# Loads, turned weights and row scales of the first layer in one block, and both square roots taken early

## The chip, the cores and the metric

The kernel runs on one core of a Trainium2 chip, as one launch. The metric is the device time of a run in microseconds (us). Five engines work side by side, each through its own list of instructions, and wait for each other through semaphores: PE (TensorE, matrix products and transposes), DVE (VectorE), ACT (ScalarE), POOL (GpSimd) and SP (SyncE, which only starts DMA transfers here). ACT starts transfers too.

## What is computed

The reference is a stack of eight layers on x of 16 sequences of 256 tokens with 128 features. Every layer begins with some normalisation of each token's row. The change lies in the beginning of the first layer, a selective state-space layer, and in the row scales that six of the layers compute. Cut to that:

```
# first layer (L0_attn_a): applied to x after a plain normalisation
mu  = mean(x, -1); var = var(x, -1)
xn  = (x - mu) * rsqrt(var + 1e-5) * norm_g + norm_b
xz  = xn @ in_w.T                       # 512 columns: x_, z
u   = silu(conv_b + causal_conv(x_, conv_w))          # 4 taps
dbc = u @ xproj_w.T                     # 64 + 16 + 16 columns
delta = softplus(dbc[:, :64] @ dt_w.T + dt_b)
A   = -exp(A_log)
h_t = exp(delta_t*A)*h_(t-1) + delta_t*B_t*u_t;  y_t = h_t . C_t
out = ((y + u*D) * silu(z)) @ out_w.T + residual
# a mixture layer later on (L0_ffn): 8 experts, chosen by feats @ centroids.T
```

A layer of this stack sees the row already normalised once (scale 1/sqrt(var+eps)) and normalises it again, so a row has two scales: `rstd`, and `rnorm`, the product of both. The second one needs the variance of the row once normalised, var/(var+1e-5), and its own root.

## The kernel before, in words

The 4096 tokens lie in 32 tiles of 128 rows (`env.X`, 128 partitions x 32 x 128). Work is written in blocks: in a block each engine has its own list, and at the block's end all engines meet in a barrier before the next block begins.

The program begins with five blocks. `launch` (L312 to L343): SP starts the eight transfers of X, four tiles each, ACT starts eight transfers of constant tables (`ident`, `identb`, `causal`, `causalT`, `ranks`, `steps`, `firsts`, `sel`; `sel` has 768 KB) and waits for them, and DVE takes each tile's statistics with bn_stats as its part lands. `row_scales` (L178 to L209, called at L471): SP starts fifteen transfers of the first layer's weights and vectors and waits for all; DVE works out the scales (`scale_rows`, L135), ACT takes the two square roots (`root_rows`, L166). A block of its own (L487 to L500): ACT forms A = -exp(A_log), DVE takes the mean off the centroids. `turn_weights` (L101 to L131): PE turns twelve pieces of the weights through `ident` into PSUM, DVE and ACT copy them out in turn. Then the first block of real work, `ma`: DVE normalises tiles into `ma_rows` (L364), PE turns them (L580) and multiplies (L588, L596, L604, L612), DVE convolves (L553, L558), ACT applies the nonlinearities.

`scale_rows` has ten steps, or seventeen with a second scale. The order before: four groups up to var+1e-5 (L139 to L146), wait for root 1, `rstd` (L148), `keep`, `shift`, then three steps that multiply the variance twice by `rstd` (L154 to L156), wait for root 2, a maximum with `floor` (L158), reciprocal (L159), `root` (L160), `rnorm` (L161). It is used in the beginning of the program, in `experts` (twice, names e_), in `begin` for `attention` (b2f) and `product_keys` (k5f and k7f), and with one scale only for rotary (r4sc) and state space (s6f). In `experts` ACT takes the roots between the copies of a loop that scores the tokens (L1278 to L1284). In `begin`, ACT takes both roots and then copies weights out of PSUM (L291).

## Time and profile before

| | us |
|---|---|
| median of 3 runs | 2678.5 (2677.33 to 2682.02) |
| profiled execution, its own time | 2683.2 |
| its span | 2681.5 |
| first tile written by `ma` begins | 30.33 |
| second expert layer begins | 1081.9 |

The profiled execution is 4.7 us above the median and 1.7 us of its time lie outside the span. Times in the rows below are from the beginning of the span. A row of the timeline is: start, time until the end of the last instruction in it, engine, line, operation, output<-inputs, how many, and in brackets how long the engine stood idle before and what ended that. SPq and ACTq are the times in which the engine's queue issued transfers.

### The profile page before, as it was taken

To read this page: it belongs to the slowest core of one execution; us is meant where nothing else is said; L and a number is where in the kernel's file an instruction comes from. 1 tells how busy PE (TensorE), PEld (TensorE's weight loads), DVE (VectorE), ACT (ScalarE), POOL (GpSimd) and SP (SyncE) were. 2 spreads that over 40 slices of the span, in tenths; PEclk is the share of its full clock that TensorE was granted. 3 is DMA by queue.
4 is the path that set the end of the run, shared out by engine and by line. 5 is a ranking of instruction groups with operands and counts; after the bars stand their busy time and mean duration, and the time that the engine had idled before them with its cause. 6 is when DMAs were issued, how large, how long until landed. Compare 5 with 4: busy or idle time off the path is not lost. (4 is left out here: it accounts for less than half of the span.)

```text
span 2681.5 us, 59371 instructions
## 1 busy us (share of the span) xinstructions
PE 2094.4 (78%) x17450; PEld 1739.1 (65%) x17451; DVE 2254.2 (84%) x5549; ACT 1864.0 (70%) x4275; POOL 1617.8 (60%) x1472
## 2 busy tenths in 40 slices
PE   4748888879599999693488877888888447888888
PEld 2336666658488888573466656777777326777777
DVE  6489999875588888656888857999999788999998
ACT  3579999756555555463255547999999349999997
POOL 0069999717300000274555547999999209999997
PEclk9869999989899999796799998999999769999999
DMA  2013333241200000111100000000000000000000
GB/s 60 3 48 97 97 96 97 72 143 52 64 1 0 0 0 1 48 52 42 41 2 0 0 1 1 0 0 0 0 0 0 1 0 1 4 8 4 4 4 8
DMA packets 67879, 70.65 MB, mean 26 GB/s; under 512 B 10408, under 2 KB 46464, under 8 KB 67648
## 3 DMA queue, kind: packets, MB, share of 16 engines
q1 hardware_dynamic: 61632, 57.56, 7.5%
q0 software_dynamic: 4992, 10.23, 1.4%
q10 hardware_dynamic: 1120, 1.22, 0.2%
q8 instruction: 65, 1.06, 0.2%
q14 instruction: 70, 0.57, 0.1%
HBM read 57.32 MB, written 11.67 MB: 26 GB/s over the span
## 5 line engine op out<-in xcount | busy, mean ns | idle before, releaser
L1899 POOL TENSOR_TENSOR k5a_psums<-k5a_sims 128x1024 f32<-128x1024 f32 x224 | 421.7, 1914 | 16.2 <-DVE k5a_w L2107 12.0
L1899 POOL TENSOR_TENSOR k7a_psums<-k7a_sims 128x1024 f32<-128x1024 f32 x224 | 421.7, 1915 | 12.9 <-DVE k7a_w L2107 8.7
L994 POOL TENSOR_TENSOR mc_hc<-mc_h,mc_cs 128x512 f32<-128x512 f32 x256 | 328.0, 1297 | 32.7 <-DVE mc_h L961 17.3
L1964 PE MATMUL k5a_pw<-g_ident,k5a_w 128*128 128x128 f32 x2048 | 265.6, 277 | 70.4 <-DVE k5a_hid L2115 45.9
L1964 PE MATMUL k7a_pw<-g_ident,k7a_w 128*128 128x128 f32 x2048 | 262.0, 276 | 70.1 <-DVE k7a_hid L2115 45.9
L1964 PEld LDWEIGHTS k5a_pw<-g_ident,k5a_w 128*128 128x128 f32 x2048 | 226.8, 141 | 113.7 <-DVE k5a_w L2107 52.7
L961 DVE TENSOR_TENSOR_SCAN mc_h<-mc_dA,mc_inj 128x512 f32<-128x512 f32 x256 | 298.5, 1200 | 2.3 <-PE mc_inj L850 1.8
L1964 PEld LDWEIGHTS k7a_pw<-g_ident,k7a_w 128*128 128x128 f32 x2048 | 227.3, 141 | 109.4 <-issue 63.8
L2107 DVE SCALAR_TENSOR_TENSOR k7a_w<-k7a_psums,k7a_best,k7a_lift 128x1024 f32<-128x1024 f32 x224 | 279.5, 1272 | 0.5 <-ACT k7a_lift L2035 0.3
L2107 DVE SCALAR_TENSOR_TENSOR k5a_w<-k5a_psums,k5a_best,k5a_lift 128x1024 f32<-128x1024 f32 x224 | 279.1, 1270 | 0.5 <-ACT k5a_lift L2035 0.3
L2035 ACT ACTIVATE k7a_lift<-k7a_psums 128x1024 f32<-128x1024 f32 x224 | 229.2, 1023 | 37.5 <-DVE k7a_w L2107 33.2
L2035 ACT ACTIVATE k5a_lift<-k5a_psums 128x1024 f32<-128x1024 f32 x224 | 228.4, 1020 | 33.3 <-DVE k5a_w L2107 28.9
L1341 POOL MEMSET e_keep<- 128x256 f32 x2 | 0.6, 312 | 407.6 <-POOLq L35 407.6
L850 PE MATMUL mc_inj<-g_ident,mc_bdu 128*128 128x128 f32 x1024 | 167.9, 287 | 58.0 <-DVE mc_h L961 53.9
L906 ACT ACTIVATE mc_bdu<-mc_duT,m_BT 128x256 f32<-128x256 f32 x384 | 178.5, 497 | 16.4 <-PE mc_inj L850 13.9
L2491 ACT ACTIVATE r4a_pr<-r4a_pst 128x384 f32<-128x384 f32 x256 | 111.6, 488 | 111.0 <-PE r4a_pst L2647 109.8
L850 PEld LDWEIGHTS mc_inj<-g_ident,mc_bdu 128*128 128x128 f32 x1024 | 109.9, 142 | 112.0 <-DVE mc_h L961 108.9
L914 ACT ACTIVATE mc_dA<-m_delta,m_A 128x510 f32<-128x510 f32 x256 | 181.2, 708 | 0.4 <-DVE mc_h L961 0.3
L2557 POOL TENSOR_SCALAR_AFFINE_SELECT r4a_pr<-r4a_pr 128x256 f32<-128x256 f32 x256 | 101.0, 412 | 110.5 <-ACT r4a_pr L2491 110.5
L1719 ACT ACTIVATE b2a_pr<-b2a_psc,b2a_nm 128x128 f32<-128x128 f32 x128 | 47.3, 369 | 158.0 <-DVE b2a_nm L1767 135.1
L857 PE MATMUL mc_yT<-g_ident,mc_hc 128*128 128x128 f32 x1024 | 153.6, 273 | 1.3 <-POOL mc_hc L994 1.1
L2764 DVE TENSOR_REDUCE r4a_nm<-r4a_work 128x2 f32<-128x512 f32 (+1 forms) x192 | 121.8, 682 | 14.0 <-PE r4a_work L2618 13.0
(515 smaller groups left out, 5869.9 us busy)
## 6 DMA issues: line engine op xcount, KB each, us to landing
mc_cs<-c_rows SPq DMA_DIRECT2D x128, 256.0 KB, 3.1
e_w<-in_L_ffn_W_dram SPq DMA_DIRECT2D x16, 256.0 KB, 5.3
token_rows<-e_zn SPq DMA_DIRECT2D x16, 256.0 KB, 3.6
e_zn<-token_out SPq DMA_DIRECT2D x16, 256.0 KB, 5.1
g_X<-in_L_attn_a_x_dram SPq DMA_DIRECT2D x8, 256.0 KB, 5.7
out_dram<-g_X SPq DMA_DIRECT2D x7, 256.0 KB, 2.3
e_zs<-token_rows,e_token POOLq DMA_INDIRECT x78, 2.6
token_out<-e_ys,e_token POOLq DMA_INDIRECT x78, 2.3
```

The costliest lines, as they stand in the source:

```text
L850: ins = nc.tensor.transpose(inj[:, q % RI, k * P:(k + 1) * P], bdu[:, S % 2, k, h * P:(h + 1) * P], env.ident[:, :])
L857: ins = nc.tensor.matmul(yT[:, n % 2, h, k * P:(k + 1) * P], rows[:, k * P:(k + 1) * P], env.ident[:, :], start=(first and k == 0), stop=( ...
L906: ins = nc.scalar.mul(bdu[:, S % 2, k, :], duT[:, n % 2, k, :], BT[:, n * TPC + k, st:st + 1])
L914: nc.scalar.activation(dA[:, q % RA, :, 1:SEQ], d[:, :, 1:SEQ], ACT.Exp, scale=A[:, h, st:st + 1]).then_inc(decay, 1)
L961: nc.vector.tensor_tensor_scan(h_[:, q % RB, :], dA[:, q % RA, :, :].rearrange("p s t -> p (s t)"), inj[:, q % RI, :], 0.0, ALU.mult, ALU. ...
L994: nc.gpsimd.tensor_tensor(hc[:, q % RH, :], h_[:, q % RB, :], cs[:, S % RC, :], ALU.mult).then_inc(outs, 1)
L1899: nc.gpsimd.tensor_tensor(psums[:, h - 1, :, :], rows_of(p, h), s2, ALU.add).then_inc(pooled, 1)
L1964: ins = nc.tensor.matmul(pw[:, j, :], w[:, h % WR, j * P:(j + 1) * P], env.ident[:, :], start=(h == 0 and j % 4 == 0), stop=(h == HD - 1 a ...
L2035: nc.scalar.activation(lift[:, h % LR, :], sums_of(h), ACT.Relu).then_inc(lifted, 1)
L2107: nc.vector.scalar_tensor_tensor(w[:, h % WR, :], sums_of(h), best[:, p, h, 7:8], lift[:, h % LR, :], ALU.is_ge, ALU.mult).then_inc(weighe ...
L2491: nc.scalar.activation(pr[:, h, :, :].rearrange("p b c -> p (b c)"), pst[:, h % 2, 0:3 * P], ACT.Exp).then_inc(expd, 1)
L2764: nc.vector.tensor_reduce(dst, src, AX, ALU.max, negate=True).then_inc(maxed, 1)
```

## The change

The five beginning blocks up to `ma` become one, `opening`. In it SP starts four parts of X, then A_log, the centroids with their two companions, dt_w, the six small vectors, then the five tables that are left; ACT starts `ident`, the other four parts of X, then in_w, xproj_w, out_w and b1. Each kind of load has its own semaphore, and each user waits for its own. `sel`, `causalT` and `root`, which nothing reads, are gone. The block waits for the weights and the small vectors; the tables are waited for at the end of `ma`. The mean of the centroids moves from DVE (a reduction and two steps) to POOL (nine steps that halve the row). PE's transposes are grouped: six places in PSUM, each copied out by ACT alone. A is formed by ACT ahead of the roots.

In `scale_rows` the variance of the normalised row is worked out as var * 1/(var+1e-5), which needs no root; these three steps stand ahead of the first wait for ACT. The maximum is left out where `floor` is zero (all but attention), `root` is left out. The steps are 15, or 16 in attention.

```diff
@@ -144,35 +144,46 @@
     link(nc.vector.scalar_tensor_tensor(t3, t1, 0.25, t1, ALU.mult, ALU.mult))
     link(nc.vector.scalar_tensor_tensor(t0, t2, 1.0 / P, t3, ALU.mult, ALU.add))
     link(nc.vector.tensor_scalar(t1, t0, 1e-5, None, ALU.add))
+    assert link.n == VARIANCE
+    if second:
+        k, eps, floor, gain = second
+        link(nc.vector.reciprocal(t3, t1))
+        link(nc.vector.tensor_tensor(t4, t0, t3, ALU.mult))
+        link(nc.vector.tensor_scalar(t0, t4, float(k), float(eps), ALU.mult, ALU.add))
+        assert link.n == SQUARES
     dve.wait_ge(rooted, 1)
     link(nc.vector.reciprocal(env.rstd[:, :], t2))
     link.inc(nc.vector.tensor_scalar(env.keep[:, :], env.rstd[:, :], 1.0, None, ALU.add))
-    link(nc.vector.scalar_tensor_tensor(env.shift[:, :], env.mean[:, :], -1.0, env.rstd[:, :],
-                                        ALU.mult, ALU.mult))
+    link.inc(nc.vector.scalar_tensor_tensor(env.shift[:, :], env.mean[:, :], -1.0, env.rstd[:, :],
+                                            ALU.mult, ALU.mult))
     if second:
-        k, eps, floor, gain = second
-        link(nc.vector.tensor_tensor(t1, t0, env.rstd[:, :], ALU.mult))
-        link(nc.vector.tensor_tensor(t3, t1, env.rstd[:, :], ALU.mult))
-        link(nc.vector.tensor_scalar(t1, t3, float(k), float(eps), ALU.mult, ALU.add))
         dve.wait_ge(rooted, 2)
-        link(nc.vector.tensor_scalar(t4, t2, float(floor), None, ALU.max))
+        if floor:
+            link(nc.vector.tensor_scalar(t4, t4, float(floor), None, ALU.max))
         link(nc.vector.reciprocal(t3, t4))
-        link.inc(nc.vector.tensor_scalar(env.root[:, :], t4, 1.0 / gain, None, ALU.mult))
-        link(nc.vector.scalar_tensor_tensor(env.rnorm[:, :], t3, float(gain), env.rstd[:, :],
-                                            ALU.mult, ALU.mult))
-    assert link.n == (17 if second else 10)
+        link.inc(nc.vector.scalar_tensor_tensor(env.rnorm[:, :], t3, float(gain), env.rstd[:, :],
+                                                ALU.mult, ALU.mult))
+    assert link.n == scale_steps(second)
+
+
+VARIANCE, SQUARES = 7, 10
...
+def scale_steps(second):
+
+    if second is None:
+        return VARIANCE + 3
+    return SQUARES + (6 if second[2] else 5)
 
 
 def root_rows(nc, act, vec, rooted, tmp, second):
 
-    t1, t2 = tmp[:, 1, :], tmp[:, 2, :]
-
-    act.wait_ge(vec, 7)
-    nc.scalar.activation(t2, t1, ACT.Sqrt).then_inc(rooted, 1)
+    act.wait_ge(vec, VARIANCE)
+    nc.scalar.activation(tmp[:, 2, :], tmp[:, 1, :], ACT.Sqrt).then_inc(rooted, 1)
     if second:
 
-        act.wait_ge(vec, 13)
-        nc.scalar.activation(t2, t1, ACT.Sqrt).then_inc(rooted, 1)
+        act.wait_ge(vec, SQUARES)
+        nc.scalar.activation(tmp[:, 4, :], tmp[:, 0, :], ACT.Sqrt).then_inc(rooted, 1)
...
+def opening(nc, env, x_dram, ident, first, rest, negated, centring, turns, tables):
...
+        def bring(eng, q):
+            eng.dma_start(env.X[:, q * G:(q + 1) * G, :], rows[:, q * G:(q + 1) * G, :]).then_inc(x_in[q], 16)
+
+        def fetch(eng, j):
+            for dst, src in first[j]:
+                eng.dma_start(dst, src, allow_slow_non_contiguous=True).then_inc(fetched[j], 16)
+
         @block.sync
         def _(sp):
-            for q in range(PARTS):
-                sp.dma_start(env.X[:, q * G:(q + 1) * G, :], rows[:, q * G:(q + 1) * G, :]).then_inc(loaded[q], 16)
+            for q in range(0, PARTS, 2):
+                bring(sp, q)
+            for j in range(1, len(first), 2):
+                fetch(sp, j)
+            for dst, src in rest:
+                sp.dma_start(dst, src, allow_slow_non_contiguous=True).then_inc(small_in, 16)
+            for dst, src in tables[1]:
+                sp.dma_start(dst, src).then_inc(tables[0], 16)
+            sp.wait_ge(small_in, 16 * len(rest))
+
+        @block.tensor
+        def _(pe):
+            pe.wait_ge(ident_in, 16)
+            for j, (ready, pieces, places) in enumerate(turns):
+                if ready is None:
+                    pe.wait_ge(centred, CENTRED)
+                    pe.wait_ge(fetched[3], 16 * len(first[3]))
+                else:
+                    pe.wait_ge(fetched[ready], 16 * len(first[ready]))
+                for src, c0 in pieces:
+                    p, f = src.shape[0], src.shape[1]
+                    ins = nc.tensor.transpose(turned[0:f, j, c0:c0 + p], src, env.ident[0:p, 0:p])
+                ins.then_inc(placed, 1)
 
...
+            act.dma_start(*ident).then_inc(ident_in, 16)
+            for q in range(1, PARTS, 2):
+                bring(act, q)
+            for j in range(0, len(first), 2):
+                fetch(act, j)
+
+            def evacuate(j):
+                act.wait_ge(placed, j + 1)
+                for dst, c0 in turns[j][2]:
+                    f, n = dst.shape[0], dst.shape[1]
+                    ins = nc.scalar.copy(dst, turned[0:f, j, c0:c0 + n])
+                ins.then_inc(evacuated, 1)
+
+            at, A = negated
+            act.wait_ge(fetched[at], 16 * len(first[at]))
+            nc.scalar.activation(A, A, ACT.Exp).then_inc(raised, 1)
+            act.wait_ge(raised, 1)
+            nc.scalar.mul(A, A, -1.0).then_inc(raised, 1)
+            act.wait_ge(vec, VARIANCE)
+            nc.scalar.activation(tmp[:, 2, :], tmp[:, 1, :], ACT.Sqrt).then_inc(rooted, 1)
+            evacuate(0)
+            act.wait_ge(vec, SQUARES)
+            nc.scalar.activation(tmp[:, 4, :], tmp[:, 0, :], ACT.Sqrt).then_inc(rooted, 1)
+            for j in range(1, len(turns)):
+                evacuate(j)
+            act.wait_ge(evacuated, len(turns))
+
+        @block.gpsimd
+        def _(pool):
+            at, cent = centring
+            link = Link(pool, centred)
+            pool.wait_ge(fetched[at], 16 * len(first[at]))
+            n = P // 2
+            link(nc.gpsimd.tensor_tensor(csum[0:E, 0:n], cent[:, 0:n], cent[:, n:2 * n], ALU.add))
+            while n > 1:
+                n //= 2
+                link(nc.gpsimd.tensor_tensor(csum[0:E, 0:n], csum[0:E, 0:n], csum[0:E, n:2 * n], ALU.add))
+            link(nc.gpsimd.tensor_scalar(csum[0:E, 0:1], csum[0:E, 0:1], 1.0 / P, None, ALU.mult))
+            link(nc.gpsimd.tensor_scalar(cent, cent, csum[0:E, 0:1], None, ALU.subtract))
+            assert link.n == CENTRED
...
         @block.vector
         def _(dve):
             for q in range(PARTS):
 
-                dve.wait_ge(loaded[q], 16)
+                dve.wait_ge(x_in[q], 16)
                 for i in range(q * G, (q + 1) * G):
                     nc.vector.bn_stats(env.stats[:, i, :], env.X[:, i, :]).then_inc(done, 1)
             dve.wait_ge(done, NT)
+            link = Link(dve, vec)
+            scale_rows(nc, env, dve, link, rooted, tmp, second)
+            link.wait()
...
+            first = [
+                [(in_w[:, :, :], a["in_w"].rearrange("(j p) c -> p j c", p=P))],
+                [(A[:, :, :], a["A_log"].rearrange("(h p) s -> p h s", p=P))],
+                [(xp[:, :], a["xproj_w"])],
+                [(rows3[0:E, :], ffn["centroids"]), (rows3[E:2 * E, :], ffn["gamma"]), (rows3[2 * E:3 * E, :], ffn["beta"])],
+                [(ow[:, :], a["out_w"])],
+                [(dtw[:, :, :], a["dt_w"].rearrange("(h p) r -> p h r", p=P))],
+                [(rows1[:, :], ffn["b1"].rearrange("e (j p) -> (e j) p", p=P))]]
...
+            turns = [
+                (0, [(in_w[:, j, :], j * P) for j in range(4)], [(wx[:, :], 0), (wz[:, :], DI)]),
+                (2, [(xp[:, h * P:(h + 1) * P], h * 96) for h in range(H)], [(xprojT[:, :, :].rearrange("p h r -> p (h r)"), 0)]),
+                (5, [(dtw[:, h, :], h * P) for h in range(H)], [(dtT[:, :], 0)]),
+                (4, [(ow[:, h * P:(h + 1) * P], h * P) for h in range(H)], [(outT[:, :, :].rearrange("p h c -> p (h c)"), 0)]),
+                (6, [(rows1[:, :], 0)], [(env.b1[:, :, :].rearrange("p e j -> p (e j)"), 0)]),
+                (None, [(rows3[:, :], 0)], [(env.byexpert[:, :, :].rearrange("p a e -> p (a e)"), 0)])]
+            opening(nc, env, a["x"], ident, first, rest, (1, A[:, :, :]), (3, rows3[0:E, :]), turns, (tabled, tables))
...
@@ -1280,8 +1354,8 @@
                     lower(n - 1)
                 if n < 2:
 
-                    act.wait_ge(scaled, (7, 13)[n])
-                    nc.scalar.activation(tmp[:, 2, :], tmp[:, 1, :], ACT.Sqrt).then_inc(rooted, 1)
+                    act.wait_ge(scaled, (VARIANCE, SQUARES)[n])
```

Three places show how the instructions move. The names behind "waits" are semaphores; a handle is reused later under its first name, so in a late layer the names say nothing of the layer.

ACT, from the end of the table loads to the first copies of turned weights. Before:

```order
L171 ACT_TABLE_LOAD
L171 ACTIVATE m_sc_tmp<-m_sc_tmp 128x32 [waits m_sc_vec]
L175 ACTIVATE m_sc_tmp<-m_sc_tmp 128x32 [waits m_sc_vec]
L185 UNCONDITIONAL_BRANCH [waits m_sc_rooted]
L487 UNCONDITIONAL_BRANCH [waits barrier_Pool_Activation_PE_DVE_SP_release]
L489 ACT_TABLE_LOAD
L489 ACTIVATE m_A<-m_A 128x32
L492 ACTIVATE m_A<-m_A 128x32 [waits mp_ma]
L486 UNCONDITIONAL_BRANCH [waits mp_ma]
L130 UNCONDITIONAL_BRANCH [waits barrier_Pool_Activation_PE_DVE_SP_release]
L122 COPY mw_wx<-m_t_turned 128x128 [waits m_t_placed]
L122 COPY mw_wz<-m_t_turned 128x128 [waits m_t_placed]
```

And after the change (m_A is A, first_tmp the scratch of the scales, first_turned the PSUM places):

```order
L394 ACT_TABLE_LOAD
L394 ACTIVATE m_A<-m_A 128x32 [waits first_fetched1]
L396 ACTIVATE m_A<-m_A 128x32 [waits first_raised]
L398 ACT_TABLE_LOAD
L398 ACTIVATE first_tmp<-first_tmp 128x32 [waits first_vec]
L389 COPY mw_wx<-first_turned 128x256 [waits first_placed]
L389 COPY mw_wz<-first_turned 128x256
L401 ACTIVATE first_tmp<-first_tmp 128x32 [waits first_vec]
L389 COPY mw_xprojT<-first_turned 128x192 [waits first_placed]
L389 COPY mw_dtT<-first_turned 64x256 [waits first_placed]
L389 COPY m_outT<-first_turned 128x256 [waits first_placed]
L389 COPY g_b<-first_turned 128x32 [waits first_placed]
```

The exponential moves ahead of the roots and has a wait for its load; the second root has the two copies of in_w's halves ahead of it and all other copies behind it.

SP at the beginning of the program. Before:

```order
L327 DMA g_X<-in_L_attn_a_x_dram 128x4x128 x8
L317 UNCONDITIONAL_BRANCH
L191 UNCONDITIONAL_BRANCH [waits barrier_Pool_Activation_PE_DVE_SP_release]
L194 DMA mp_in_w<-in_L_attn_a_in_w_dram 128x4x128
L194 DMA mw_cw<-in_L_attn_a_conv_w_dram 128x2x4
L194 DMA mp_xp<-in_L_attn_a_xproj_w_dram 96x256
L194 DMA mp_dtw<-in_L_attn_a_dt_w_dram 128x2x64
L194 DMA mp_ow<-in_L_attn_a_out_w_dram 128x256
L194 DMA m_A<-in_L_attn_a_A_log_dram 128x2x16
L194 DMA m_convb<-in_L_attn_a_conv_b_dram 128x2x1
L194 DMA m_dtb<-in_L_attn_a_dt_b_dram 128x2x1
L194 DMA m_Dd<-in_L_attn_a_D_dram 128x2x1
```

And after the change:

```order
L345 DMA g_X<-in_L_attn_a_x_dram 128x4x128 x4
L349 DMA m_A<-in_L_attn_a_A_log_dram 128x2x16
L349 DMA mp_rows<-in_L_ffn_centroids_dram 8x128
L349 DMA mp_rows<-in_L_ffn_gamma_dram 8x128
L349 DMA mp_rows<-in_L_ffn_beta_dram 8x128
L349 DMA mp_dtw<-in_L_attn_a_dt_w_dram 128x2x64
L358 DMA m_g<-in_L_attn_a_norm_g_dram 128x1
L358 DMA m_b<-in_L_attn_a_norm_b_dram 128x1
L358 DMA mw_cw<-in_L_attn_a_conv_w_dram 128x2x4
L358 DMA m_convb<-in_L_attn_a_conv_b_dram 128x2x1
L358 DMA m_dtb<-in_L_attn_a_dt_b_dram 128x2x1
L358 DMA m_Dd<-in_L_attn_a_D_dram 128x2x1
```

There is no barrier between X and the weights, and A_log and the centroids stand right behind SP's half of X.

DVE in the last product-key layer (k7f), from the end of the first variance to the first row of work. Before:

```order
L146 TENSOR_SCALAR k7f_tmp<-k7f_tmp 128x32 [waits first_loaded1]
L148 RECIPROCAL g_rstd<-k7f_tmp 128x32 [waits first_loaded0,first_loaded1]
L149 TENSOR_SCALAR g_keep<-g_rstd 128x32 [waits first_loaded1]
L150 SCALAR_TENSOR_TENSOR g_shift<-g_mean,g_rstd 128x32
L154 TENSOR_TENSOR k7f_tmp<-k7f_tmp,g_rstd 128x32 [waits first_loaded1]
L155 TENSOR_TENSOR k7f_tmp<-k7f_tmp,g_rstd 128x32 [waits first_loaded1]
L156 TENSOR_SCALAR k7f_tmp<-k7f_tmp 128x32 [waits first_loaded1]
L158 TENSOR_SCALAR k7f_tmp<-k7f_tmp 128x32 [waits first_loaded0,first_loaded1]
L159 RECIPROCAL k7f_tmp<-k7f_tmp 128x32 [waits first_loaded1]
L160 TENSOR_SCALAR g_root<-k7f_tmp 128x32 [waits first_loaded1]
L161 SCALAR_TENSOR_TENSOR g_rnorm<-k7f_tmp,g_rstd 128x32
L236 TENSOR_SCALAR k7f_rows<-g_X,g_mean,g_rnorm 128x128 [waits first_loaded1]
```

And after the change:

```order
L146 TENSOR_SCALAR k7f_tmp<-k7f_tmp 128x32 [waits first_xin0]
L150 RECIPROCAL k7f_tmp<-k7f_tmp 128x32 [waits first_xin0]
L151 TENSOR_TENSOR k7f_tmp<-k7f_tmp 128x32 [waits first_xin0]
L152 TENSOR_SCALAR k7f_tmp<-k7f_tmp 128x32 [waits first_xin0]
L155 RECIPROCAL g_rstd<-k7f_tmp 128x32 [waits m_tabled,first_xin0]
L156 TENSOR_SCALAR g_keep<-g_rstd 128x32 [waits first_xin0]
L157 SCALAR_TENSOR_TENSOR g_shift<-g_mean,g_rstd 128x32
L163 RECIPROCAL k7f_tmp<-k7f_tmp 128x32 [waits m_tabled]
L164 SCALAR_TENSOR_TENSOR g_rnorm<-k7f_tmp,g_rstd 128x32 [waits first_xin0]
L249 TENSOR_SCALAR k7f_rows<-g_X,g_mean,g_rnorm 128x128 [waits first_xin0]
```

The three steps that feed the second root stand ahead of `rstd`, the maximum and `g_root` are gone.

## Rows read from the trace of the kernel before

**Rows 1.** The page's busy time, share of the span and instructions of each engine.

```profile
PE 2094.4 (78%) x17450; PEld 1739.1 (65%) x17451; DVE 2254.2 (84%) x5549; ACT 1864.0 (70%) x4275; POOL 1617.8 (60%) x1472
```

**Rows 2.** Timeline, all engines, 0 to 20 us: loads of X and row scales.

```profile
0.81 5.27 SPq L327 DMA_DIRECT2D g_X<-in_L_attn_a_x_dram  x8
...
4.15 0.87 DVE L342 BATCH_NORM_STATS2 g_stats<-g_X 128x6 f32<-128x128 f32 x4 [4.01 <-DMA g_X<-in_L_attn_a_x_dram]
...
14.07 1.65 DVE L342 BATCH_NORM_STATS2 g_stats<-g_X 128x6 f32<-128x128 f32 x8 [2.99 <-DMA g_X<-in_L_attn_a_x_dram]
...
16.26 0.21 DVE L139 TENSOR_TENSOR m_sc_tmp<-g_stats 128x32 f32<-128x32 f32 x1 [0.54 <-PEq L317]
...
17.51 0.23 ACT L171 ACTIVATE m_sc_tmp<-m_sc_tmp 128x32 f32<-128x32 f32 x1
...
20.24 0.18 DVE L161 SCALAR_TENSOR_TENSOR g_rnorm<-m_sc_tmp,g_rstd 128x32 f32<-128x32 f32 x1
```

**Rows 3.** Timeline, all engines, 22 to 46 us: last load, A, turned weights, first tile.

```profile
22.76 0.32 SPq L194 DMA_DIRECT2D mp_rows<-in_L_ffn_b_dram  x1
24.65 1.28 ACT L489 ACT_TABLE_LOAD   x1 [5.21 <-PEq L185]
...
29.54 0.19 ACT L122 COPY g_b<-m_t_turned 128x32 f32<-128x32 f32 x1
30.33 2.14 DVE L364 TENSOR_SCALAR ma_rows<-g_X,g_mean,g_rnorm 128x128 f32<-128x128 f32 x8 [0.72 <-PEq L370]
```

**Rows 4.** Windows: stretch, engines' busy time (count), clock, DMA share, GB/s.

```profile
3.00:4.50 1.50, 0.00 (x0) 0.00 (x0) 0.35 (x2) 0.00 (x0) 0.00 (x0) 1.00 1.17 334
...
10.50:12.00 1.50, 0.00 (x0) 0.00 (x0) 0.58 (x4) 0.00 (x0) 0.00 (x0) 1.00 1.01 255
```

**Rows 5.** Groups by line and form: count, busy us, mean ns, idle before.

```profile
L1709 ACT COPY b2a_qT<-b2a_pq 128x256 f32<-128x256 f32 x128 | 47.4, 370 | 1.8 <-PE b2a_pq L1637 1.2
...
L1910 POOL TENSOR_TENSOR k7a_cand<-k7a_top 128x96 f32<-128x96 f32 x32 | 11.5, 359 | 0.0
...
L2886 POOL TENSOR_TENSOR state_space_bias<-state_space_bb 128x2 f32<-128x2 f32 x1 | 0.2, 188 | 0.0
```

**Rows 6.** Timeline, all engines, scales of the last product-key layer.

```profile
2197.17 0.35 DVE L148 RECIPROCAL g_rstd<-k7f_tmp 128x32 f32<-128x32 f32 x1 [0.38 <-ACT k7f_tmp L171]
2197.56 0.18 DVE L149 TENSOR_SCALAR g_keep<-g_rstd 128x32 f32<-128x32 f32 x1
2197.65 0.18 DVE L150 SCALAR_TENSOR_TENSOR g_shift<-g_mean,g_rstd 128x32 f32<-128x32 f32 x1
2197.87 0.19 DVE L154 TENSOR_TENSOR k7f_tmp<-k7f_tmp,g_rstd 128x32 f32<-128x32 f32 x1
```

**Rows 7.** Timeline, all engines, the first product-key layer.

```profile
1610.09 0.23 ACT L175 ACTIVATE k5f_tmp<-k5f_tmp 128x32 f32<-128x32 f32 x1 [1.47 <-DVE k5f_tmp L156]
1610.22 0.58 ACT L291 ACTIVATE k5g_keysT<-k5f_wide 128x512 f32<-128x512 f32 x1
...
1610.86 4.47 PE L268 MATMUL k5f_wide<-k5g_keysT,product_keys_wq 128*128 128x32 f32 x20 [0.93 <-ACT k5g_keysT L291]
```

**Rows 8.** Timeline, attention's beginning: PE's last turn of rows.

```profile
725.06 0.66 PE L280 MATMUL b2f_tp<-g_ident,b2f_rows 128*128 128x128 f32 x4 [0.37 <-DVE b2f_rows L236]
```

**Rows 9.** Timelines, both expert layers: second roots, and DVE's wait for the scores.

```profile
558.84 0.23 ACT L1284 ACTIVATE e_tmp<-e_tmp 128x32 f32<-128x32 f32 x1 [0.53 <-DVE e_tmp L156]
...
570.88 0.42 DVE L1403 TENSOR_REDUCE e_mx<-e_ph 128x32 f32<-128x256 f32 x1 [2.24 <-PE e_ph L1159]
...
1086.24 0.23 ACT L1284 ACTIVATE e_tmp<-e_tmp 128x32 f32<-128x32 f32 x1 [0.48 <-DVE e_tmp L156]
```

**Rows 10.** Timeline of PE in `ma`, at its beginning and near its end.

```profile
33.49 3.78 PE L588 MATMUL ma_px<-ma_zc,mw_wx 128*128 128x512 f32 x4 [0.87 <-ACT ma_zc L646]
...
38.99 1.98 PE L588 MATMUL ma_px<-ma_zc,mw_wx 128*128 128x512 f32 x4
...
102.67 3.33 PE L604 MATMUL ma_pr<-m_u,mw_xprojT 128*96 128x512 f32 x4 [1.92 <-issue]
```

## What the change does to the time: a prediction

> **What bounds the kernel now.** The page comes first: DVE is busy for 84% of the span [rows 1], and no engine for all of it, so the question is which wait ends last in each of the places that the change touches. The beginning comes next, in the timeline. DVE's statistics wait for X, whose last two parts are there at 14.07 us, and end at 15.72; the scales run from 16.26 to 20.42 [rows 2]. Meanwhile SP issues fifteen transfers, the last from 22.76 on, and only at 24.65 does the next block begin, so the weights' loads set that end, not the scales; A, the centroids and the turned weights follow and ACT's last copy ends at 29.73; `ma` writes its first tile at 30.33 [rows 3]. All of this is in a row: none of these 30.33 us has a stage beside it. In these rows three barriers lie between things that need not follow each other. The later layers come last. There, the two roots sit in the scales with waits at both, and what that costs depends on who waits behind them.
>
> **The beginning.** X is 2.10 MB, with `ident` 2.16 MB. The DMA engines moved 334 GB/s in the best window shown and 255 GB/s later [rows 4]; the flow begins at about 2.4 us by an estimate: the first part of X, 0.26 MB, is there at 4.15 [rows 2] and with as much of the tables beside it takes 1.8 us at the middle rate of 290. Before, 1.2 MB of tables shared these rates with X. After the change only `ident` goes ahead, and the weights stand behind X in the same queues. At 290 GB/s, the middle, X has landed at 2.4 + 7.4 = 9.9 us; at the two ends at 8.9 and 10.9. The splitting over two queues is costed at nothing: SP issued all of X by 6.08 [rows 2], long before it had landed. DVE needs 0.87 us for four tiles, 7.0 for all, so from a first pair at about 4.5 it can't end before 11.5; from the last pair at 9.9 with 1.65 us for eight tiles [rows 2] it would end at 11.55. I take **11.7**, with 11.4 and 15.7 as ends (the latter if X is no earlier than before).
>
> Then the scales, with no barrier ahead. From the first step to root 1 it was 1.25 us [rows 2], so root 1 is at 11.8 + 1.25 = 13.05. The new order of DVE's steps by their distances: a reciprocal holds the next dependent step for 0.39 us (2197.17 to 2197.56), another dependent step for 0.22 (2197.65 to 2197.87), an independent one for 0.09 [rows 6]. These hold for all layers, since the steps take 128 x 32 numbers everywhere. After the seventh step: reciprocal 0.39, two steps 0.44, `rstd` 0.39, `keep` and `shift` 0.19, reciprocal 0.39, `rnorm` 0.2, in all 2.0: DVE is done at about 15.1. Root 2 can start 0.8 after root 1 and is needed 1.4 after it, so DVE waits for no root.
>
> ACT from root 1 on: two roots of 0.23, four copies of 256 or 192 columns at about 0.37 [rows 5] plus one more of that size, and two small ones of 0.19 [rows 3]: 2.7 us end to end, 1.9 with the 0.1 by which neighbours overlap in the rows. I take 2.3 and get **15.4** for the end of ACT, later than DVE. What must be there by then: the other weights, 0.58 MB behind X, landed at 9.9 + 2.0 = 11.9 at 290 GB/s and 13.2 at 255; PE's twelve transposes and their copies took less than the 3.8 us from the end of the table load at 25.93 to 29.73 [rows 3] and lie before that, group by group as their weights land. POOL's nine steps aren't in the trace; the nearest rows are 188 ns for 2 columns and 359 for 96 [rows 5], with 0.1 us for the wait in each that makes 2.6 to 4.1 us after the centroids at about 10.5, so 13.1 to 14.6, ahead of the last copy's turn at 15.2 but by little. I put it at nothing and keep 0.5 us for it in the range. SP's six small vectors are issued by about 8.7 (eleven more issues at some 0.5 after four parts of X) and land before 13. The exponential and its table load move onto ACT ahead of root 1: A_log lands at about 10.5, two activations of 0.23 and one table load of 1.28 [rows 3] end at 12.3, 0.7 before root 1 is due, so hidden; with A_log at 11.5 it costs 0.3.
>
> The Trainium skill, "ScalarE: Activation LUTs", section "What ACT_TABLE_LOAD costs", speaks against this order: a switch of tables costs 1.28 us for the load and about 1.38 more to drain, some 2.66 in all. By that, an estimate from the Trainium skill, root 1 would be at 13.7 instead of 13.05 and the gain 0.6 us smaller; in the trace's table loads the next activation starts where the 1.28 us end, and the sum goes by these.
>
> From ACT's last copy to the first tile it was 0.6 us [rows 3]. So `ma` begins at 15.4 + 0.6 = 16.0 instead of 30.33: **14.3 us** less, with ends at 10.3 (X as late as before) and 15.2.
>
> **The scales in the later layers.** Before, `rnorm` starts 3.98 us after the first step (16.26 to 20.24 [rows 2]); by the distances above it is 1.25 + 0.39 + 0.44 + 0.39 + 0.19 + 0.39 = 3.05 now. In k7f, whose weights are already made, PE and ACT have nothing to do but DVE's rows, so the difference of 0.9 us is all on the path; its steps stand at the same distances [rows 6]. In k5f DVE's rows have slack behind PE's products, but these wait 0.93 us for ACT's copy of the keys, which stands behind root 2, for which ACT stood idle 1.47 us [rows 7]. Root 2 comes 0.9 earlier, and the copy with it: 0.9, its other end 0 if PE's products don't follow. In attention the maximum stays, so the chain is 0.22 longer than in k7f and saves 0.7; PE's last turn waits 0.37 us for DVE [rows 8], so DVE's rows set the end, and I take 0.6. In the expert layers DVE waits 2.24 us for the scores after its rows, so shorter scales are worth nothing there. The scoring loop itself has ACT idle for 0.53 and 0.48 us before root 2 [rows 9], which goes, since its input is now ready before root 1 is taken: 0.5 each. Root 1 stands where it stood. The layers with one scale don't change. Sum of the later layers: 0.9 + 0.9 + 0.6 + 0.5 + 0.5 = **3.4 us**, with ends at 0.9 and 4.
>
> The sum is 14.3 + 3.4 = 17.7 us. The profiled execution would go from 2683.2 to 2665.5, the median from 2678.5 to **2660.8**.
>
> **The rivals.** (a) X is not earlier. Splitting X over two queues and putting small transfers behind it could let weights flow between its parts. Before, the last two parts came 3 us after the others while a table of 768 KB was under way [rows 2], so mixing does delay X; but this table is gone and 0.58 MB stand behind. If X's last part lands at 12 to 14, the whole gains 2 to 4 us less: 2663 to 2665. (b) The later layers give nothing, as other waits take the place of the roots: 2678.5 - 14.3 = 2664. Speaking for it are the slack of DVE in the experts, against it ACT's idle times. (c) No change that can be measured: the 14 us come back at a later wait. That would need a stage bound by something that runs on its own from the program's beginning, such as the tables, waited for at the end of `ma`. They are 0.3 MB and issued by about 12 us, while `ma` before was still at work at 102.67 [rows 10]: no row speaks for it. (d) Slower than before: PE's clock. In `ma` four products of L588 took 3.78 us at first and 1.98 later, and near the end four of L604 took 3.33 [rows 10]: the lower level of 1.2 GHz against 2.4. Before, PE turned weights right ahead of `ma`; now these transposes are spread over some microseconds and PE idles before the block. If the clock stays at the lower level in `ma`, each of the eight chunks costs up to about 7 us more: four such groups of products (L588, L596, L604, L612, with as many columns each), each 1.8 us longer; from three chunks on the gain is gone, and with four more than at present the time is 2678.5 - 17.7 + 28 = 2689. Against it: before, the clock also rose only after 3.5 us of products in `ma`, and I see no reason that it won't again.
>
> **How the numbers follow.** The forecast itself (gain of 15 to 20 us): 0.62. (a) 0.13, (b) 0.15, (c) 0.04, (d) at full size 0.03, and 0.03 for a gain over 20, as the stages' clock may rise a little earlier or later in each of the layers. The range holds the first three and the bounds of the unknown costs: 2678.5 less 11.5 and less 22.5 gives **2656 to 2667**; widening the upper end by 1 for the runs' own spread of some 2 us gives 2668. 0.2% is 5.4 us, about what a measurement of this kernel can tell from no change: faster 0.93, same 0.04, slower 0.03.
>
> **What would show it.** In the profile after: the last statistics end at 11.5 to 12; root 1 at 13, root 2 less than 1.3 us later; ACT's last copy ends at 15 to 16 and the first tile of `ma` starts near 16.0; if that is at 18 or more, the row with the longest wait before it tells whether X, POOL or the small vectors were late. In k7f `rnorm` starts 3.1 us after the first step. ACT's idle time before root 2 in the experts is zero. The distance from the first tile of `ma` (30.33 [rows 3]) to the end of the span of 2681.5 is 2651.2 before and should be 2647.8. The prediction is wrong if this distance grows, or if the first tile starts after 20.

## The result, and the profile after

| | before | after |
|---|---|---|
| median, us | 2679.48 (2677.33 to 2682.02, 4 runs) | 2666.25 (2664.41 to 2669.44, 4 runs) |
| profiled span, us | 2681.5 | 2664.6 |
| first tile of `ma` | 30.33 | 16.44 |
| from there to the span's end | 2651.2 | 2648.1 |

The ratio is 0.9949, with an interval of 0.9934 to 0.9963: 13 to 14 us faster (10 to 18 by the interval), where 17.7 were forecast. The time of 2666.25 lies in the range of 2656 to 2668, near its upper end. The kernel was run twice more beside other kernels: 0.9945 [0.9932, 0.9959] and 0.9950 [0.9938, 0.9963].

The page's busy times of after (busy us, share, instructions) answer to [rows 1]. Hardly anything has changed: the gain is not in work left out.

```profile
PE 2092.7 (79%) x17450; PEld 1738.0 (65%) x17451; DVE 2249.4 (84%) x5529; ACT 1863.0 (70%) x4276; POOL 1620.6 (61%) x1481
```

The timeline of after, all engines, 0 to 17 us, answers to [rows 2, 3].

```profile
0.81 2.11 SPq L345 DMA_DIRECT2D g_X<-in_L_attn_a_x_dram  x4
1.29 2.37 ACTq L345 DMA_DIRECT2D g_X<-in_L_attn_a_x_dram  x4
...
4.22 0.87 DVE L426 BATCH_NORM_STATS2 g_stats<-g_X 128x6 f32<-128x128 f32 x4 [4.09 <-DMA g_X<-in_L_attn_a_x_dram]
...
6.03 1.64 DVE L426 BATCH_NORM_STATS2 g_stats<-g_X 128x6 f32<-128x128 f32 x8 [0.94 <-DMA g_X<-in_L_attn_a_x_dram]
...
8.40 4.08 DVE L426 BATCH_NORM_STATS2 g_stats<-g_X 128x6 f32<-128x128 f32 x20 [0.73 <-DMA g_X<-in_L_attn_a_x_dram]
...
10.58 0.23 ACT L396 ACTIVATE m_A<-m_A 128x32 f32<-128x32 f32 x1
10.83 1.28 ACT L398 ACT_TABLE_LOAD   x1
...
11.54 1.64 POOL L415 TENSOR_TENSOR first_csum<-first_csum 8x32 f32<-8x32 f32 x6
12.52 0.21 DVE L139 TENSOR_TENSOR first_tmp<-g_stats 128x32 f32<-128x32 f32 x1
...
13.62 0.62 POOL L417 TENSOR_SCALAR mp_rows<-mp_rows,first_csum 8x128 f32<-8x128 f32 x1
...
13.79 0.23 ACT L398 ACTIVATE first_tmp<-first_tmp 128x32 f32<-128x32 f32 x1 [1.67 <-DVE first_tmp L146]
...
14.61 0.23 ACT L401 ACTIVATE first_tmp<-first_tmp 128x32 f32<-128x32 f32 x1
...
15.55 0.18 ACT L389 COPY g_byexpert<-first_turned 128x24 f32<-128x24 f32 x1
15.58 0.19 DVE L164 SCALAR_TENSOR_TENSOR g_rnorm<-first_tmp,g_rstd 128x32 f32<-128x32 f32 x1
16.44 2.14 DVE L451 TENSOR_SCALAR ma_rows<-g_X,g_mean,g_rnorm 128x128 f32<-128x128 f32 x8 [0.67 <-PEq L457]
```

What to see: DVE waits for X three times (4.09, 0.94, 0.73) and never after 8.40. From there it does 20 tiles in 4.08 us without a gap, so that the end of the statistics, 12.48, is set by two late parts at the beginning and then by DVE's own pace; but only just, since the last part of X landed no earlier than 11.3 (its rows stand under "Statistics, 11.7" below). Root 1 had waited 1.67 us for DVE: exponential, table load and weights are all covered. At the end ACT (15.73) and DVE (15.77) are done together.

### The profile page after: what moved, and what is told of

It is laid out like the page before. It is cut to its first block and busy times, and to the rows that moved or that the text cites. A ratio compares the mean times of both kernels' runs of the same rounds, so it can differ in the third digit from the quotient of the medians.

```text
span 2664.6 us, 59310 instructions
## 1 busy us (share of the span) xinstructions
PE 2092.7 (79%) x17450; PEld 1738.0 (65%) x17451; DVE 2249.4 (84%) x5529; ACT 1863.0 (70%) x4276; POOL 1620.6 (61%) x1481
## 5 line engine op out<-in xcount | busy, mean ns | idle before, releaser
L1973 POOL TENSOR_TENSOR k5a_psums<-k5a_sims 128x1024 f32<-128x1024 f32 x224 | 421.6, 1913 | 17.3 <-DVE k5a_w L2181 12.0
L1973 POOL TENSOR_TENSOR k7a_psums<-k7a_sims 128x1024 f32<-128x1024 f32 x224 | 421.7, 1914 | 13.9 <-DVE k7a_w L2181 8.7
L2109 ACT ACTIVATE k7a_lift<-k7a_psums 128x1024 f32<-128x1024 f32 x224 | 229.2, 1023 | 37.6 <-DVE k7a_w L2181 33.2
L980 ACT ACTIVATE mc_bdu<-mc_duT,m_BT 128x256 f32<-128x256 f32 x384 | 178.3, 497 | 16.7 <-PE mc_inj L924 14.3
L2838 DVE TENSOR_REDUCE r4a_nm<-r4a_work 128x2 f32<-128x512 f32 (+1 forms) x192 | 122.2, 683 | 14.3 <-PE r4a_work L2692 13.2
```

What stands on the lines that cost most here:

```text
L980: ins = nc.scalar.mul(bdu[:, S % 2, k, :], duT[:, n % 2, k, :], BT[:, n * TPC + k, st:st + 1])
L1973: nc.gpsimd.tensor_tensor(psums[:, h - 1, :, :], rows_of(p, h), s2, ALU.add).then_inc(pooled, 1)
L2109: nc.scalar.activation(lift[:, h % LR, :], sums_of(h), ACT.Relu).then_inc(lifted, 1)
L2838: nc.vector.tensor_reduce(dst, src, AX, ALU.max, negate=True).then_inc(maxed, 1)
```

## Where in the program the gain lies

The next table is worked out from the profiles, in us: the distances between the first rows of the stages. "rest" is from the first tile of `ma` to the end of the span. The edits of the kernels are in the next section.

| kernel | `ma` begins | attention to 2nd experts | k5f's first row to the first products of k5a | k7f's the same, to k7a | k7f to end | rest |
|---|---|---|---|---|---|---|
| before | 30.33 | 369.5 | 19.00 | 14.81 | 485.9 | 2651.2 |
| scales alone | 30.5 | 368.8 | 18.13 | 13.79 | 485.8 | 2648.3 |
| opening alone | 17.3 | 370.8 | 19.01 | 14.81 | 486.0 | 2652.7 |
| after | 16.4 | 368.8 | 18.32 | 13.79 | 485.8 | 2648.1 |
| after, again | 16.3 | 368.8 | 18.32 | 13.79 | 485.8 | 2652.8 |
| after, a third time | 16.2 | 368.8 | 18.54 | 13.79 | 485.8 | 2653.5 |
| before, again | 30.5 | 369.5 | 19.01 | 14.81 | 485.9 | 2648.5 |

The last column warns of a trap. Before and after differ by 3.1 us in it, close to the forecast 3.4, but the second profile of before reads 2648.5 and the second of after 2652.8, the other way round. So the prediction's sign of being wrong, that this distance grows, can't be read from one pair of profiles. Profiles of one kernel lie 2.6 to 5.4 us apart there, mostly in stages that the change leaves alone. Only short stages, bounded by rows that the change touches, tell of single microseconds, and there the profiles of one kernel agree within 0.1 to 0.3 us.

## The experiments

**The opening alone: the new opening block, the old scales in all layers.**

```diff
-    assert link.n == VARIANCE
-    if second:
-        k, eps, floor, gain = second
-        link(nc.vector.reciprocal(t3, t1))
...
     dve.wait_ge(rooted, 1)
...
+    if second:
+        k, eps, floor, gain = second
+        link(nc.vector.tensor_tensor(t1, t0, env.rstd[:, :], ALU.mult))
+        link(nc.vector.tensor_tensor(t3, t1, env.rstd[:, :], ALU.mult))
...
```

> This is the changed kernel with the row scales and the places of the roots as they were before, everywhere (also in the opening block). Theory A (the time comes from the opening, by its parts): the first tile of ma starts about 0.9 us later than in the changed kernel (16.44), so near 17.3 us, and the whole gains about 13 us against the kernel before: ratio near 0.9951. Theory B (the later layers' scales bring a good part of it): the ratio is at 0.997 or above, since only part of the gain is left.

**The scales alone: the five blocks of before, the new scales.** The edit is the part of the diff in `scale_rows`, `root_rows` and the experts' root, on the kernel before.

> This is the kernel before with the new row scales alone, the beginning in its five blocks. Theory A: in the beginning the scales hide behind SP's loads, so the first tile of ma stays at 30.3 us; attention's block is 0.8 us shorter, the beginnings of both product-key layers 0.7 to 0.9 us each, the expert layers not at all: gain of 0 to 2.5 us, ratio 0.9990 to 1.0000. Theory B: the gain of 16.9 us in the span has 3 us or more from the scales: ratio 0.9988 or lower. Theory C (PE's clock takes it back at the start of each product-key layer): ratio 1.0000, with the first two products of L1936 at 2.1 us instead of 1.1.

**After and before, unaltered, beside them.**

> The changed kernel a second time. Theory A (the rotary layer's 4.6 us less and the second expert layer's 2.0 us more are the clock's phase, not the change): these two stretches come out differently by 1 to 4 us from the first profile, 361.7 and 160.8 us, while the first tile of ma stays within 0.3 us of 16.44. Theory B (they follow from the change): both lie within 0.5 us of the first profile. The ratio should be 0.993 to 0.996 in either.

> The kernel before a second time, for the lengths of its stretches. Theory A: rotary 366.3 and second expert layer 158.8 us change by 1 to 4 us, and the first tile of ma stays at 30.3. Theory B: all within 0.5 us.

Measured: opening alone 2671.82 us, ratio 0.9957 [0.9944, 0.9971]; scales alone 2680.71, 0.9993 [0.9984, 1.0002]; after 2668.21, 0.9945 [0.9932, 0.9959]; before 2682.64 in this comparison, and 2680.77 in its profiled execution. The opening is worth 11.5 us (8 to 15 by its interval), with the first tile at 17.3 as its theory A had it. The scales alone can't be told from no change, and their interval allows 0 to 4 us. Their profile bears out theory A for attention (0.8 us shorter) and for the first products of k5a (0.9 earlier, 1.12 us long), and theory C for k7a, whose first two products take 2.07 us instead of 1.12. In the new opening they have one more place: the first tile of `ma` is at 17.3 with the old ones and at 16.2 to 16.4 with the new, whereas in the old opening they were worth nothing (30.5), since SP's loads set the end there, as was argued from [rows 3]. Of the stretches that the expectations name, the rotary layer takes 366.0 us in after's second profile (361.7 in the first) and 364.8 in before's (366.3), the second expert layer 160.0 (160.7) and 157.5 (158.8): the rotary layer's 4.6 us less are not the change's, and of the expert layer's 2.0 more nothing is shown.

**X over one queue.**

```diff
-            for q in range(0, PARTS, 2):
+            for q in range(PARTS):
                 bring(sp, q)
...
-            for q in range(1, PARTS, 2):
-                bring(act, q)
```

> The changed kernel with one edit: all eight parts of X are issued by SP, none by ACT. In the changed kernel's profile X's parts were issued by 2.4 us and the statistics ended at 12.48, with DVE busy without a wait from 8.40 on. Theory 1 (the split over two queues costs and gains nothing, since the DMA engines' rate sets X's landing): SP's eighth issue ends near 4.5 us, long before the data has flowed; statistics end at 12.2 to 12.8, first tile of `ma` at 16.2 to 16.8, time within 0.5 us. Rival (the split is what brings X's first parts early, since each queue serves its parts one after the other): the first statistics start later than 4.22 by up to 1 us, DVE waits between the parts, statistics end at 13 to 14 and all after them moves along, +0.6 to +1.5 us.

Measured: 2666.68 us, ratio 0.9952 [0.9936, 0.9969]; the statistics end at 13.07 and `ma` begins at 17.25. The timeline of DVE in this kernel, and one row of PE:

```profile
5.28 0.87 DVE L424 BATCH_NORM_STATS2 g_stats<-g_X 128x6 f32<-128x128 f32 x4 [0.30 <-DMA g_X<-in_L_attn_a_x_dram]
...
7.19 0.87 DVE L424 BATCH_NORM_STATS2 g_stats<-g_X 128x6 f32<-128x128 f32 x4 [1.04 <-DMA g_X<-in_L_attn_a_x_dram]
...
8.60 4.47 DVE L424 BATCH_NORM_STATS2 g_stats<-g_X 128x6 f32<-128x128 f32 x20 [0.54 <-DMA g_X<-in_L_attn_a_x_dram]
...
16.13 0.30 PE L374 MATMUL first_turned<-g_ident,mp_rows 24*128 24x24 f32 x1 [1.67 <-POOL mp_rows L415]
```

The rival's end is right, at the lower end of its sizes, but not the way to it: the first statistics start at 4.10, no later than in after (4.22). What the profile shows is that with ACT's queue free of X, `in_w` and `xproj_w` flow beside X, are turned from 6.02 on already, and the waits for X grow from 1.67 to 1.88 us with 0.4 more in the last 20 tiles. SP's eight issues also took until 6.98 instead of the 4.5 expected, so the centroids came later too: POOL worked on them from 13.00 to 16.08, PE waited 1.67 us for it, and ACT's last copy ended at 16.64, 0.1 after DVE. The split was costed at nothing; here it is worth 0.8 us in the opening, too little for the medians to show.

**The table of 768 KB back, on ACT's queue ahead of its parts of X.** (The expectation below says "behind ACT's four parts of X"; in the kernel the table stands right behind `ident` and so ahead of them. Neither of its two theories was worked out for that place.)

```diff
             act.dma_start(*ident).then_inc(ident_in, 16)
+            act.dma_start(*tables[2]).then_inc(tables[0], 16)
             for q in range(1, PARTS, 2):
                 bring(act, q)
...
+        env.sel = sb("sel", [96, 32, P], BF16)
...
```

> The changed kernel, but the table of 768 KB is loaded again, on ACT's queue right behind `ident` and so behind ACT's four parts of X and ahead of the weights. It tells how much of the earlier statistics (15.72 before, 12.48 now) comes from taking tables out of X's way. Theory 1 (transfers queued behind X still share the engines with X's last parts, and the weights behind get later by their bytes): 768 KB at 290 GB/s are 2.7 us; the weights and A_log land up to 2.7 us later, X itself 0 to 2 later; since root 1 waited 1.67 us for DVE and PE's first transposes wait for weights, the first tile starts at 17.5 to 19.5, time +1 to +3 us. Rival (all that the table costs is behind X and hidden, since DVE is the bound from 8.40 on): first tile at 16.3 to 17, time within 0.5 us.

Measured: 2669.37 us, ratio 0.9961 [0.9946, 0.9977], 2.7 us above the kernel with one queue beside it, though the two intervals overlap; the first tile of `ma` at 20.4, 3.9 later than after. The timeline of DVE and PE:

```profile
4.18 0.87 DVE L427 BATCH_NORM_STATS2 g_stats<-g_X 128x6 f32<-128x128 f32 x4 [4.04 <-DMA g_X<-in_L_attn_a_x_dram]
...
10.15 1.65 DVE L427 BATCH_NORM_STATS2 g_stats<-g_X 128x6 f32<-128x128 f32 x8 [5.10 <-DMA g_X<-in_L_attn_a_x_dram]
...
13.90 2.42 DVE L427 BATCH_NORM_STATS2 g_stats<-g_X 128x6 f32<-128x128 f32 x12 [0.26 <-DMA g_X<-in_L_attn_a_x_dram]
...
16.13 1.09 PE L374 MATMUL first_turned<-g_ident,mp_in_w 128*128 128x128 f32 x4 [16.13 <-DMA mp_in_w<-in_L_attn_a_in_w_dram]
```

The table is not hidden in this place: the statistics end at 16.32, later than the 15.72 of before. Whether it would be hidden behind X, as the rival has it, stays untested. Three quarters of a megabyte ahead of half of X hold the second part of X back by 4 us (DVE waits 5.10 instead of 0.94), more than the 2.7 us that its own bytes take at 290 GB/s. Together with the run before it, in which SP alone issues X as in the kernel before and the statistics still end at 13.07, this speaks for the tables as the greater part of X's delay before: X is early because of what no longer stands in or beside its way. No run has the five old blocks without the tables, so how much of it the table of 768 KB alone is worth isn't shown.

**Spare work on ACT in the experts' scoring loop.**

```diff
                 if n < 2:
...
+                elif n < 6:
+                    nc.scalar.activation(spare[:, n - 2, :], env.ident[:, 0:32], ACT.Sqrt)
```

> The changed kernel with four spare square roots of 128x32 (0.23 us each, 0.9 in all) on ACT in the scoring loop of each expert layer, one in each of chunks 2 to 5. Theory (the loop goes at TensorE's pace of 1.88 us per chunk, and ACT has 0.35 + 0.37 us of idle time in each, so the idle 0.53 and 0.48 us before root 2 were worth nothing): from TensorE's first e_pz to ACT's last copy of the scores it stays 15.8 us in the first expert layer (541.17-541.50 less, to 556.18) within 0.3, and the chunks stay 1.88 apart. Rival (ACT's copies are on the path, and the gain of 0.5 us per layer was there and lost elsewhere): 0.9 us longer in each of the two layers, chunks 2.1 apart where the spare roots stand.

Measured: 2665.96 us in one run. The timeline of ACT in the first expert layer:

```profile
545.26 0.57 ACT L1348 COPY e_st<-e_po 8x512 f32<-8x512 f32 x1 [0.37 <-PE e_po L1228]
545.74 0.23 ACT L1361 ACTIVATE e_spare<-g_ident 128x32 f32<-128x32 f32 x1
546.19 0.58 ACT L1353 COPY e_zc<-e_pz 128x512 f32<-128x512 f32 x1 [0.22 <-PE e_pz L1249]
547.14 0.57 ACT L1348 COPY e_st<-e_po 8x512 f32<-8x512 f32 x1 [0.37 <-PE e_po L1228]
```

The copies stay 1.88 us apart (545.26 to 547.14; in the second expert layer 1073.10 to 1074.98). ACT's idle time shrinks from 0.35 to 0.22 and takes the root in. From the first copy to the last it is 541.22 to 555.97 = 14.75 us, without the spare roots 541.50 to 556.18 = 14.68, and before 555.24 to 569.80 = 14.56. The theory holds: idle time of ACT is worth nothing in this loop.

**Dummy transposes ahead of the two places with a low clock.**

```diff
             pe.wait_ge(ident_in, 16)
+            for _ in range(28):
+                nc.tensor.transpose(spare[:, 0:P], env.ident[:, :], env.ident[:, :])
...
                 front.credit(pe)
+                for _ in range(5):
+                    nc.tensor.transpose(pg[:, 0:P], env.ident[:, :], env.ident[:, :])
...
+            if inner and not weights:
+                for _ in range(18):
+                    nc.tensor.transpose(wide[:, 0, 0:P], env.ident[:, :], env.ident[:, :])
```

> The changed kernel with dummy transposes of `ident` on TensorE where it would wait: 28 in the opening, 5 at the beginning of `ma`, 18 at the beginning of k7f. They write to PSUM that nobody reads. Theory (TensorE's clock is low in both places because it waited before them, and what the shorter scales of k7f save, 0.95 us, was given back since the first products of k7a now run at the lower level): in `ma` the first four products of L661 take 1.9 instead of 3.78 us and the first chunks end 3 to 8 us earlier; in k7a the two products of 512 columns take 1.12 instead of 2.08 us, and the distance from the first row of k7f to the span's end becomes 484.9 or less instead of 485.8 to 486.1 (six profiles of four kernels). Whole time 3 to 7 us under the changed kernel's. Rival (the clock follows something that dummy work in front doesn't change, or the clock is given but DVE and ACT bound the chunks): the four products stay at 3.78, or get faster while the second chunk starts no earlier; the time is within 1 us, k7f to end stays at 485.8, or the dummies get into the way and it is up to 1 us longer.

Measured: 2667.69 us, ratio 0.9951 [0.9938, 0.9965]. The four products stay at 3.78 us, the two of k7a at 2.07, k7f to end at 485.8: the rival's numbers. The windows of this kernel (busy us of PE, PEld, DVE, ACT, POOL with counts, granted clock, DMA share, GB/s) show when:

```profile
12.00:14.00 2.00, 1.79 (x11) 1.21 (x11) 1.83 (x10) 0.35 (x2) 1.49 (x5) 0.75 0.97 195
14.00:16.00 2.00, 0.39 (x3) 0.26 (x2) 1.46 (x8) 1.54 (x8) 0.00 (x0) 0.50 0.00 0
...
22.00:24.00 2.00, 2.00 (x8) 1.17 (x7) 1.10 (x3) 0.22 (x1) 0.00 (x0) 0.69 0.00 0
24.00:26.00 2.00, 2.00 (x6) 0.87 (x5) 2.00 (x5) 1.86 (x3) 0.00 (x0) 1.00 0.00 0
```

The clock was at 2.4 GHz when the weights were turned (four transposes of `in_w` in 0.66 us, against 1.09 after) and fell within 12 to 14 us. PE had just stood idle for 2.3 us, waiting for `in_w`; the next run shows that this wait by itself doesn't make the clock fall.

**Dummy transposes throughout; and after a third time.**

```diff
+            dummies(nc, env, spare[:, 0:P], 40)
...
                 ins.then_inc(placed, 1)
+                dummies(nc, env, spare[:, 0:P], 2)
+            dummies(nc, env, spare[:, 0:P], 2)
...
+                dummies(nc, env, pg[:, 0:P], 7)
                 turn(0, 0)
+                dummies(nc, env, pg[:, 0:P], 5)
...
                 ins.then_inc(turned, 1)
+                if inner and not weights:
+                    dummies(nc, env, wide[:, 0, 0:P], 2)
...
+                dummies(nc, env, pmix[:, 0:P], 8)
                 sim(0, 0)
```

(`dummies` issues that many transposes of `ident`; the 18 at the beginning of k7f are as above.)

> The changed kernel with dummy transposes of `ident` that leave TensorE hardly an idle time, in the three places where its clock was low: in the opening 40 ahead of the weights, two behind each group and two at the end; at the beginning of `ma` 7 ahead of the first chunk's transposes and 5 ahead of its projections; in k7f 18 at first and two behind each chunk; in k5a and k7a 8 ahead of the first products. In the run with dummies at the beginnings alone the granted clock was high ahead of both places and fell again at 13.0 us and at 13.9 us after k7f's first row, in or right behind stretches where TensorE was busy for 0.2 to 0.8 of the time. Theory (it is TensorE's idle time just ahead that lets the clock fall): the first four products of `ma` take 1.9 to 2.2 us, the first two of k7a and k5a 1.1, k7f to end is 484.9 instead of 485.8; all in all 3 to 4 us less than the changed kernel's time on the same chip. Rival (the clock falls regardless, or it falls at the change of blocks in which TensorE has to idle for 0.6 us and more): the products stay at 3.78 and 2.08, k7f to end at 485.8, the time within 1 us.

> The changed kernel a third time, unaltered, on the same chip as the kernel without idle times on TensorE, to compare with. Both theories: 2666 to 2668 us, first tile of `ma` at 16.3 to 16.5, k7f to end 485.8 to 485.9, the four products of L661 at 3.78 us.

Measured: 2663.82 us (2658.98 to 2667.48), ratio 0.9940 [0.9927, 0.9952]; after beside it 2667.42, 0.9950 [0.9938, 0.9963], with its first tile at 16.2, 0.1 earlier than expected, and the rest as expected. The timeline of PE with dummies throughout:

```profile
12.50 0.66 PE L385 MATMUL first_turned<-g_ident,mp_in_w 128*128 128x128 f32 x4 [2.23 <-DMA mp_in_w<-in_L_attn_a_in_w_dram]
...
16.38 0.96 PE L99 MATMUL ma_pg<-g_ident 128*128 128x128 f32 x7 [0.45 <-PEq L341]
...
19.06 1.98 PE L674 MATMUL ma_px<-ma_zc,mw_wx 128*128 128x512 f32 x4 [0.32 <-ACT ma_zc L734]
...
22.35 1.98 PE L674 MATMUL ma_px<-ma_zc,mw_wx 128*128 128x512 f32 x4
...
2192.69 1.02 PE L2025 MATMUL k7a_pmix<-k5g_G,k7a_zc 128*128 128x512 f32 x2
```

And of after:

```profile
19.59 3.78 PE L661 MATMUL ma_px<-ma_zc,mw_wx 128*128 128x512 f32 x4 [0.87 <-ACT ma_zc L719]
...
25.23 1.88 PE L661 MATMUL ma_px<-ma_zc,mw_wx 128*128 128x512 f32 x4
...
2192.54 2.08 PE L2010 MATMUL k7a_pmix<-k5g_G,k7a_zc 128*128 128x512 f32 x2 [1.52 <-ACT k7a_zc L2076]
```

The first four products of `ma` now run at 2.4 GHz, and the second chunk's projections begin 2.9 us earlier (22.35 against 25.23). From the first tile of `ma` to the first expert layer it is 521.4 us, against 523.0 to 525.3 in eleven other profiles. From k7f's first row (2178.31) to the end it is 485.3, against 485.6 to 486.0 in all others, half of the 0.95 that was expected. The other half went to the dummies: the eight ahead of the products held these back to 14.4 us after k7f's first row, 0.6 later than the 13.8 of after.

The kernel isn't free of idle times. PE waited 2.23 us for `in_w` here too, nearly as long as the 2.32 of the run before, and the clock did not fall. So more spare work holds the clock, but which idle time lets it fall, or whether it takes several, isn't shown. The medians differ by 3.6 us, as the theory has it, but their intervals overlap: the profile shows the faster products, the total is only likely.

## Why the prediction was right, point by point

**The total.** The range held, the forecast itself didn't: a gain of 15 to 20 us had 0.62, and the three comparisons give 13 to 15 us by their ratios, 11 to 14 by their medians. The beginning came out nearly as added up; of the 3.4 us for the later layers most did not come. The range held because its upper end had left room for rivals (a) and (b).

**Statistics, 11.7.** Measured 12.48, within the ends given (12.28 and 12.14 in the other two profiles of after). X's rate was right: from 2 to 10 us the engines moved 244, 309, 288 and 277 GB/s in steps of 2 us, 2.24 MB in all. Its landing was not. The sum had X there at 9.9, with 10.9 as the late end; the last part was issued at 3.06 and landed 8.3 us later, at 11.3 (rows of the timeline and of the DMA issues, in KB and us to landing):

```profile
3.06 0.61 ACTq L345 DMA_DIRECT2D g_X<-in_L_attn_a_x_dram  x1
...
g_X<-in_L_attn_a_x_dram ACTq DMA_DIRECT2D x1, 256.0 KB, 8.3
```

From 2 to 11.34 us the engines moved 2.56 MB at 274 GB/s, 0.4 MB more than X and `ident` have, so other loads flowed between X's parts: rival (a), in the small. With 0.87 us for four tiles the statistics couldn't end before 12.2. The other 0.3 is what the sum put at nothing: DVE also waited for two early parts (0.94 and 0.73), and 4.22 + 0.94 + 0.73 with 6.59 us of work (0.87 + 1.64 + 4.08) give 12.48.

**Root 1, 1.25 after the first step.** Measured 12.52 to 13.79, 1.27. The rule of the Trainium skill, "ScalarE: Activation LUTs", "What ACT_TABLE_LOAD costs", had 1.38 us of drain beside the 1.28 of the load. No row here shows it, and the rows decide: the activation of 0.23 us begins at 10.58 and the load at 10.83, 0.02 behind its end; in the second expert layer the copy ends at 1069.17, the load begins at 1069.18 and the root at 1070.48, 0.02 behind the load.

```profile
1068.58 0.59 ACT L1352 COPY e_zc<-e_pz 128x512 f32<-128x512 f32 x1 [3.66 <-PE e_pz L1248]
1069.18 1.28 ACT L1358 ACT_TABLE_LOAD   x1
1070.48 0.23 ACT L1358 ACTIVATE e_tmp<-e_tmp 128x32 f32<-128x32 f32 x1
1070.61 0.57 ACT L1352 COPY e_zc<-e_pz 128x512 f32<-128x512 f32 x1
```

In the opening the load had ended at 12.11, 1.7 us before root 1 was due, so by an estimate from that page's 1.38 us the order would have stood the drain too.

**ACT's and DVE's ends, 15.4 and 15.1.** After root 1, DVE took 1.98 (2.0 forecast) and ACT 1.94 (2.3 forecast); both start 0.7 late with the statistics, and end together. **POOL, hidden**: 11.15 to 14.24, 3.1 us, in its range of 2.6 to 4.1, and 0.8 ahead of PE's turn of its rows (15.05). **The other loads**: by their times to landing, in_w was there at 12.7 and the last of the weights at 13.7, where 11.9 to 13.2 were put, and the last small vector at 14.2 instead of before 13. Both were hidden all the same, as ACT's copies begin behind root 1, at 13.98, and DVE and ACT end at 15.8. **First tile 0.6 after**: 0.67. The sum of 14.3 for the beginning came out as 13.9, missed by the 0.8 of the statistics, less the 0.4 that ACT was quicker. That nothing runs beside these stages is borne out: the opening alone begins `ma` 13.0 earlier and takes 11.5 less in all (8 to 15). (The upper end of 15.2 for the beginning is 0.2 more than its terms give: 0.3 for the statistics and 0.4 for ACT make 15.0.)

**k7f, 0.9.** The scales are shorter as forecast (`rnorm` starts 3.05 after the first step), and the first products of k7a come 1.0 earlier in the profiles with the new scales (0.4 with dummies throughout). Yet k7f to end goes from 485.9 to 485.8 only. The timelines of PE before and after:

```profile
2210.38 1.12 PE L1936 MATMUL k7a_pmix<-k5g_G,k7a_zc 128*128 128x512 f32 x2 [1.52 <-ACT k7a_zc L2002]
```

```profile
2192.54 2.08 PE L2010 MATMUL k7a_pmix<-k5g_G,k7a_zc 128*128 128x512 f32 x2 [1.52 <-ACT k7a_zc L2076]
```

The two products take 0.96 longer, nearly the whole gain: ACT's third copy into k7a_zc is 34.22 us after k7f's first row, where it was 34.28. The windows show the granted clock, of before from 2210.40 on and of after from 2192.60 on:

```profile
2210.40:2212.40 2.00, 2.00 (x10) 1.33 (x10) 0.18 (x2) 0.95 (x4) 0.19 (x1) 1.00 0.05 12
```

```profile
2192.60:2194.60 2.00, 2.00 (x3) 0.97 (x4) 0.00 (x0) 0.08 (x1) 0.00 (x0) 0.50 0.01 4
```

The prediction's "all on the path" failed here: what came earlier ran at the other clock. It is no accident of one profile: in the eight profiles with the new scales and without the dummies throughout, the two products take 1.86 to 2.08 us, and in the three with the old scales 1.12, 1.13 and 1.43. It is rival (d), in the small and in another place than it was put. With dummies throughout, the products took 1.02.

**k5f, 0.9.** In the scales alone the first products of k5a come 0.9 earlier, at the high clock (1.12), and ACT's third copy into k5a_zc still does (37.6 us after k5f's first row instead of 38.5). In after they come 0.7 earlier at 2.08, that copy is at 38.75, and the gain is gone. So this gain depends on where the clock happens to stand.

**Attention, 0.6.** 369.5, 369.5 and 370.8 with the old scales, 368.7 to 368.8 in the nine profiles with the new: about 0.8. Right.

**The experts, 0.5 each.** Wrong, and this step failed in its reasoning, not in a size: ACT's idle time before root 2 did go, as the prediction's own sign of success had it (the root at 1071.61 has no idle time), but the loop did not become shorter: from ACT's first copy e_zc of the first expert layer to DVE's first row of the scores it is 15.6 and 16.5 us in the two profiles of before, 15.8, 16.1 and 16.3 in the three of after. DVE's wait for the scores only grew; the rows of after, first and second expert layer:

```profile
557.26 0.42 DVE L1477 TENSOR_REDUCE e_mx<-e_ph 128x32 f32<-128x256 f32 x1 [3.44 <-PE e_ph L1233]
```

```profile
1085.17 0.42 DVE L1477 TENSOR_REDUCE e_mx<-e_ph 128x32 f32<-128x256 f32 x1 [4.38 <-PE e_ph L1233]
```

Against [rows 9] the first wait is 1.2 us longer. PE sets the pace with 1.88 us per chunk, as the spare roots showed.

**The sum.** Beginning 13.9; attention 0.8; k5f 0 to 0.9; k7f and experts 0: 14.7 to 15.6 where 17.7 stood. The measured ratios of the three comparisons, 0.9945 to 0.9950, are 13 to 15 us. The steps that failed are two: the 0.5 us in each expert layer, where ACT was taken to be on the path, and the 0.9 in k7f and k5f, where the products were taken to keep their clock. Of the rivals, (a) holds in part (the statistics 0.8 late), (b) mostly, (c) not at all.

## What to carry to other kernels

Idle time of an engine before an instruction is a gain only if that engine sets the loop's pace; look at the next iterations of the same loop, where ACT's waits of 0.35 and 0.37 us for PE in each chunk would have told it. When a chain ahead of the matrix products is shortened by about a microsecond, read the granted clock at the place where they will then fall. And bytes in front of a load can cost more than their own time where that load feeds an engine in parts (4 us for 2.7 here): look for a big table in its way before reshaping blocks.

## What the runs showed of the hardware

TensorE's clock fell from 2.4 to 1.2 GHz around stretches in which it was only partly busy: in after the window from 2189 to 2191 us has 1.46 us of PE and the clock at 1.00, that from 2191 to 2192 has 0.02 and 1.00, and from 2192.60 on it is at 0.50. In before a like stretch left it high: from 2208 to 2210.40 PE was busy for 0.67 us, and the products behind ran at 1.00. With dummies throughout it stayed high in the opening and ahead of k7a's first products, over a wait of 2.23 us in the opening. What makes it fall in one of these stretches and not in another isn't shown. In the profile of after the granted clock reads 1.00 all through the first 40 us, although the four products at 19.59 took 3.78 us, twice the 1.88 of those at 25.23. With dummies, where the clock had changed once before, the same products at the same 3.78 us stand at 0.50. So at the start of a profile the durations have to be trusted, not the clock's column.

What stays open: what lets the clock fall; how the opening's gain divides between the tables, the barriers and the order of the loads, of which only the order was varied by runs; whether the gain of 3.6 us with dummies throughout is all real, since two medians 0.13% apart are hardly told apart by five and six runs; and what moves the 2 to 5 us between two profiles of one kernel in the stages that nothing touched.
